# State products with g's high and low parts stacked on the partitions, half-row time order, and new instruction orders on all five queues

## The reference, cut to what matters

```python
x = x + (einsum('bnh,boh->bno', x, W[subject]) + b[subject])                 # layer 0
h = relu(x @ W1[lang] + b1[lang]); y = x + h @ W2[lang] + b2[lang]
x = x + layernorm(y) * gamma[lang] + beta[lang]                              # layer 1
# layer 2
ctx   = causal_ema(x, tau_ctx)
gated = x * sigmoid([x, ctx] @ Wg.T + bg)
h1    = gelu(x @ Wn1.T + bn1)
mod   = 0.5 + sigmoid(h1 @ Wn2.T + bn2)                                      # 32 values d per time
traces = vmap over d: causal_ema(gated * mod[d], tau[d])
temporal = sum_d softmax(blend)[d] * traces[d]
out = (gelu(x @ Wsoma.T + bsoma) * sigmoid(temporal @ Wtemp.T + btemp)) @ Wout.T
x = x + layernorm(out) * gamma2 + beta2
# layer 3: x = x + zX * (row second difference) + zY * (time second difference) + zR * x * (1 - x)
```

## Time and profile before

| | |
|---|---|
| Time, median of 3 runs | 1044.95 us (1042.16 to 1045.16) |
| Profiled execution, its own time | 1038.77 us |
| Span in that profile | 1037.0 us |
| Mean granted TensorE clock | 0.97 of full |
| TensorE, matrix products busy | 919.3 us, 89% |
| VectorE busy | 831.4 us, 80% |
| ScalarE busy | 392.7 us, 38% |
| GpSimd busy | 615.0 us, 59% |

### The profile page before, as it was taken

The page is one execution under the profiler, slowest core; times in us unless marked ns, Lnnn a source line. Parts: engine busy times, 40 slices in busy tenths (PEclk is TensorE's granted clock), DMA queues, the critical chain, the costliest instruction groups (busy, mean ns, idle before and its releaser), DMA issues.

```text
span 1037.0 us, 18886 instructions
## 1 busy us (share of the span) xinstructions
PE 919.3 (89%) x6088; PEld 776.7 (75%) x6088; DVE 831.4 (80%) x1333; ACT 392.7 (38%) x730; POOL 615.0 (59%) x654
## 2 busy tenths in 40 slices
PE   2678899999899999999999999999999999998961
PEld 1458697878778787878878787887878787887751
DVE  3788779797978979798888979698887969697762
ACT  3463433434243443434343342425343343424220
POOL 1445447484756668484766749475766748474523
PEclk9779999999999999999999999999999999999985
DMA  6664333534343343534454353434344353420011
GB/s 218 214 212 137 108 123 111 165 107 155 115 153 133 116 163 108 158 118 135 129 146 132 122 168 105 155 102 162 124 131 154 104 161 114 141 72 32 31 41 61
DMA packets 92815, 133.28 MB, mean 129 GB/s; under 512 B 15692, under 2 KB 32588, under 8 KB 92716
## 3 DMA queue, kind: packets, MB, share of 16 engines
q1 hardware_dynamic: 88372, 125.93, 38.9%
q10 hardware_dynamic: 4344, 6.14, 1.9%
HBM read 106.86 MB, written 8.39 MB: 111 GB/s over the span
## 4 chain that ended last, share of the span: by engine, by line
DVE 33%; issue 24%; POOL 19%; PE 16%; ACT 3%; DMA 2%; SPq 1%; ACTq 1%; POOLq 0%; DVEq 0%
PE bank L1241 6%; DVE work L998 5%; PE bank L1371 4%; DVE w_r L829 4%; POOL work L416 4%; POOL xh L391 3%; DVE work L1007 3%; POOL b_t L403 2%; PE bank L1233 2%; POOL work L452 2%; DVE work L1014 2%; DMA w_land<-in_L_cond_weight 2%; DVE amath L975 2%; DVE work L1068 2%; POOL work L457 2%
## 5 line engine op out<-in xcount | busy, mean ns | idle before, releaser
L416 POOL TENSOR_TENSOR work<-work 128x448 f32<-128x448 f32 (+3 forms) x224 | 200.3, 894 | 35.4 <-DVE work L998 18.5
L1241 PE MATMUL bank<-x2h,wg_r 128*128 128x256 f32 x1536 | 198.2, 284 | 12.8 <-DVE bank L946 12.8
L1241 PEld LDWEIGHTS bank<-x2h,wg_r 128*128 128x128 f32 x1536 | 185.8, 188 | 27.3 <-DVE bank L946 16.9
L1371 PE MATMUL bank<-gh,amath 128*128 128x512 f32 x384 | 106.1, 412 | 21.7 <-DVE work L998 17.2
L998 DVE TENSOR_TENSOR work<-bank,work 128x512 f32<-128x512 f32 (+7 forms) x256 | 105.1, 446 | 19.5 <-POOL work L416 14.0
L1233 PE MATMUL bank<-w_r,xh 128*128 128x512 f32 x384 | 106.2, 415 | 15.6 <-DVE w_r L829 11.3
L403 POOL TENSOR_TENSOR b_t<-b_t,work 128x512 f32<-128x512 f32 x32 | 51.8, 1618 | 107.9 <-DMA b_t<-in_L_cond_b 66.0
L1241 PE MATMUL bank<-x2h,wsoma_r 128*128 128x256 f32 x768 | 107.5, 289 | 3.7 <-ACT work L615 3.5
L1371 PEld LDWEIGHTS bank<-gh,amath 128*128 128x128 f32 x384 | 68.0, 190 | 55.6 <-DVE amath L975 16.3
L829 DVE TENSOR_TENSOR w_r<-w_land,w_r 128x1024 fp32r<-128x1024 f32 x64 | 85.5, 1337 | 26.6 <-ACT w_r L542 26.6
L1241 PEld LDWEIGHTS bank<-x2h,wsoma_r 128*128 128x128 f32 x768 | 94.4, 188 | 12.7 <-issue 7.2
(11 more groups left out here) (142 smaller groups left out, 1651.1 us busy)
## 6 DMA issues: line engine op xcount, KB each, us to landing
w_land<-in_L_cond_weight SPq DMA_DIRECT2D x64, 512.0 KB, 3.9
w_t<-in_L_cond_W SPq DMA_DIRECT2D x64, 256.0 KB, 3.2
work<-work SPq DMA_DIRECT2D x64, 224.0 KB, 2.5
work<-in_xT SPq DMA_DIRECT2D x32, 256.0 KB, 3.5
b_t<-in_L_cond_bias SPq DMA_DIRECT2D x32, 256.0 KB, 3.5
work<-in_x SPq DMA_DIRECT2D x32, 256.0 KB, 3.4
work<-in_L_cond_beta SPq DMA_DIRECT2D x32, 256.0 KB, 3.5
b_t<-in_L_cond_b SPq DMA_DIRECT2D x32, 256.0 KB, 3.3
```

The costliest lines, as they stand in the source:

```text
L416: g_.tensor_tensor(dst, dst, src, ALU.add).then_inc(S["acc_ready"], 1)
L1241: ins = mm(dst, weight[:, w_part, first_block + a, o * P:(o + 1) * P], act[:, x_part, a], start=(not onto and a + w_part + x_part == 0), s ...
L1371: ins = mm(STATES[r][s_][:, :], amath[:, a_part, s_ * P:(s_ + 1) * P], gh[:, g_part], start=(a_part + g_part == 0), stop=(a_part == 1))
```

## The change

**Time order.** Inside a row the 128 times were ordered by place in the chunk (8), then by chunk (16). Now each half row of 64 times has this order by itself: half (2), place in the chunk (8), chunk (8). All access patterns that turn one order into the other get one more level, and chunk terms are worked on as 8 runs of 8 x (8 - j) elements in place of 4 runs of 16 x (8 - j).

**States.** The states of groups 0 and 1 depend on the first 64 times only, which now are partitions 0 to 63. So `gh` gets a third part: its upper 64 partitions hold g's high part and its lower 64 the low part, both of the first half. The lower half of `amath`'s high part gets a second copy of its upper half for these two groups. One product over 128 partitions is then high x high plus high x low, and a second one over 64 partitions is low x high. Groups 2 and 3 stay as they were. ACT gets three new instructions per row: `g_top` and `g_bottom` (64 x 512) and `amat_dup` (64 x 256).

**Memory.** `h1T` and `m` share a buffer now, so `mod_hidden` on ACT has two more waits, and the reserved DMA scratch is 256 in place of 1024.

**Orders.** The lists of calls on all five queues are written anew.

```diff
+    HALVES = 2
+    KH = NK // HALVES
+    HT = T // HALVES
...
-        h1T, m_q = buf("h1T"), buf("m")
+        h1T = buf("h1T")
+        m_q = h1T
...
-        gh = sb("gh", [P, 2, C], f32r)
+        gh = sb("gh", [P, 3, C], f32r)
...
+            def g_top(p, r):
+                act.wait_ge(S["ghi_ready"], 2 * p + r + 1)
+                if 2 * p + r:
+                    act.wait_ge(S["state_done"], NG * (2 * p + r) - 2)
+                a_.activation(gh[0:P // 2, 2], gh[0:P // 2, 0].bitcast(f32), ACT.Copy).then_inc(S["gtop_ready"], 1)
+
+            def g_bottom(p, r):
+                act.wait_ge(S["glo_ready"], 2 * p + r + 1)
+                if 2 * p + r:
+                    act.wait_ge(S["state_done"], NG * (2 * p + r) - 2)
+                a_.activation(gh[P // 2:P, 2], gh[0:P // 2, 1].bitcast(f32), ACT.Copy).then_inc(S["gbottom_ready"], 1)
+
+            def amat_dup(p, r):
+                act.wait_ge(S["amathi_ready"], 2 * p + r + 1)
+                a_.activation(amath[P // 2:P, 0, 0:2 * P], amat[0:P // 2, 0:2 * P], ACT.Copy).then_inc(S["amatdup_ready"], 1)
...
             def state_weights_lo(p, r):
-                dve.wait_ge(S["amathi_ready"], 2 * p + r + 1)
+                dve.wait_ge(S["amatdup_ready"], 2 * p + r + 1)
...
                 for j in W_TILES[w]:
-                    width = NK * (Q - j)
-                    src = RING[n % 2][:, at_:at_ + 4 * width].rearrange("p (a r t) -> p a r t", a=2, r=2)
+                    width = KH * (Q - j)
+                    src = RING[n % 2][:, at_:at_ + 8 * width].rearrange("p (x t) -> p x t", x=8)
...
-                for a_part, g_part in ((0, 0), (0, 1), (1, 0)):
-                    ins = mm(STATES[r][s_][:, :], amath[:, a_part, s_ * P:(s_ + 1) * P], gh[:, g_part],
-                             start=(a_part + g_part == 0), stop=(a_part == 1))
+                cols_ = slice(s_ * P, (s_ + 1) * P)
+                if s_ == 0:
+                    pe.wait_ge(S["gtop_ready"], b + 1)
+                    pe.wait_ge(S["gbottom_ready"], b + 1)
+                if s_ < 2:
+                    mm(STATES[r][s_][:, :], amath[:, 0, cols_], gh[:, 2], start=True, stop=False)
+                    ins = mm(STATES[r][s_][:, :], amath[0:P // 2, 1, cols_], gh[0:P // 2, 0], start=False, stop=True)
+                else:
+                    for a_part, g_part in ((0, 0), (0, 1), (1, 0)):
+                        ins = mm(STATES[r][s_][:, :], amath[:, a_part, cols_], gh[:, g_part],
+                                 start=(a_part + g_part == 0), stop=(a_part == 1))
```

On SP, the calls behind `shift_rows(i, 0)` in a step are now these:

```diff
                     if live(i):
                         shift_rows(i, 0)
                     if live(i + 3):
-                        load_b0(i + 3, 0)
+                        load_b1(i + 3, 0)
+                        load_w1(i + 3, 0)
                         load_x(i + 3, 0)
```

More of the change, by code:

```diff
@@ L504, in _ @@
                 if live(i):
+                    quadratic(i, 0)
+                if live(i + 1):
+                    add_terms(i + 1, 9)
+                if i == -3:
+                    mask_spread()
+                if live(i + 3):
+                    x_plus_beta(i + 3, 0)
+                if live(i):
                     rstd(mv_c, rs_c, 2, i, 1)
                 if live(i + 3):
-                    x_plus_beta(i + 3, 0)
+                    x_lo(i + 3, 1)
+                if live(i):
+                    neighbours(i, 1)
+                if live(i + 3):
+                    x1_plus_b2(i + 3, 0)
                 if live(i + 2):
                     x2_plus_beta(i + 2, 1)
+                if live(i + 3):
+                    rstd(mv_a, rs_a, 1, i + 3, 0)
+                if live(i):
+                    row_neighbours(i, 1)
+                if live(i + 3):
+                    x_plus_b0(i + 3, 1)
+                if live(i):
+                    quadratic(i, 1)
+                if live(i + 3):
+                    x_plus_beta(i + 3, 1)
+                    x1_plus_b2(i + 3, 1)
+                if live(i + 2):
+                    add_terms(i + 2, 2)
+                    add_terms(i + 2, 3)
         @block.scalar
@@ L706, in _ @@
                     x1_turned(i + 2, 1)
-                if live(i + 3):
-                    w0_hi(i + 3, 0, 0)
                 if live(i + 1):
                     mod_rows(i + 1)
+                    amat_hi(i + 1, 0)
+                if i == -3:
+                    logs()
+                if live(i + 1):
+                    amat_dup(i + 1, 0)
                 if live(i + 2):
                     relu(i + 2, 1)
+                if i == -1:
+                    hi_parts(4)
+                if live(i + 3):
+                    x_hi(i + 3, 0)
+                if live(i + 1):
+                    soma_gelu(i + 1, 2)
+                    g_hi(i + 1, 0)
+                if live(i + 2):
+                    x2_hi(i + 2, 0)
+                if live(i + 1):
+                    soma_gelu(i + 1, 3)
+                    g_top(i + 1, 0)
+                    g_bottom(i + 1, 0)
+                if live(i + 3):
+                    w0_hi(i + 3, 0, 1)
+                if i == -3:
+                    exps()
+                if live(i + 2):
+                    x2_turned(i + 2, 0)
+                if live(i + 1):
+                    amat_hi(i + 1, 1)
+                    g_hi(i + 1, 1)
+                    amat_dup(i + 1, 1)
                 if i == -2:
@@ L1202, in _ @@
                 if live(i + 2):
-                    y_row(i + 2, 1)
+                    y_stats(i + 2, 1)
                 if live(i + 1):
-                    state_weights_lo(i + 1, 0)
-                    chunk_terms(i + 1, 6)
+                    g_lo(i + 1, 0)
                 if live(i + 2):
-                    y_stats(i + 2, 1)
+                    y_aggregate(i + 2, 1)
+                if live(i + 1):
+                    chunk_terms(i + 1, 8)
+                if live(i + 2):
+                    x2_lo(i + 2, 0)
+                    centred(i + 2, 1)
                 if live(i):
@@ L1478, in _ @@
                     tn_turn(i + 1, 1)
+                if i == -3:
+                    blend_rows()
                 if i == -2:
```

495 lines of the change are left out of this document (233 added, 262 removed).

## The result

The changed kernel takes 1067.6 us, median of 4 runs (1064.69 to 1068.75), against 1043.56 us (1039.01 to 1045.16) for the kernel before on the same chip: ratio 1.0233, 95% interval 1.0193 to 1.0274. It is slower by 2.3%; 1022 was forecast, and the range ended at 1057.

The account below looks back on a forecast made before the run. The prediction took a loop of TensorE (95% busy), VectorE and a side chain as the bound. A pair going from 58.96 to 57.4 us saves 1.56, times 15 = 23 us, from 1044.95: 1022 us, range 1010 to 1034 (8 in 10: 1001 to 1057).

Parts of the forecast that it names:

- third stretch: Row 0's `x3_row` to the next `temporal`: 13.9 us by the side chain, longer than VectorE's 13.1.
- side chain: Beside the third stretch: shifts, load of x, `x_plus_b0`, `quadratic`, last add, copy and turn ahead of `temporal`; 13.9 us.
- first stretch: Row 0's `temporal` to `y_row`, set by TensorE: 12.2 us against 10.77, one more `gate_ctx` standing ahead of the adapter.
- second stretch: VectorE's other work, between the first stretch and the third stretch: 29.3 us, with 0.6 of short waits 29.9.
- loop: The three stretches of a pair added up: 12.2 + 29.9 + 13.9 = 56.0 us.
- slower rival: Array shape changes in groups 0 and 1 cost 0.36 us each: 1074 us; chance 0.18, with smaller slips 0.21.
- my two signs of under 0.4 and of 1.4: Both first groups' time over 4 products: under 0.4 us more as forecast, 1.4 us if the slower rival holds.
- (a): Both last chunk weights ahead of `project`: 12 products cover the chunk terms, taking most of TensorE's 1.1 us a pair.
- (b): `final_sum` of row 1 behind all scans: VectorE's 2.7 us and TensorE's 0.8 us of idle time a pair go.
- moved wait: Shifts held by a load ahead of them, `temporal` waits for the last add: loop 57.5, 1044 us; chance 0.12.
- Start and tail: The span outside the repeated pairs, 152.6 us: no sure change, left at 0, give or take 5 us.
- the 1.4 us that I left idle: Half of TensorE's 2.9 us of idle time a pair, left on top of the loop: 57.4 us a pair.

Follow-up runs that it names:

- e4: The changed kernel with the load of x issued on SP right behind row 0's shifts, ahead of the loads of b1 and w1: 1025.57 us, ratio 0.9870.
- e6: e4 with the second stacked product over all 128 rows, the lower half of `amath`'s low part being zero: 1020.92 us, ratio 0.9809.
- e5: e4 with three products in the first two state groups and without the copies of g's parts: 1025.88 us, ratio 0.9842.
- e7: The changed kernel with the last add of the chunk terms ahead of `row_neighbours` and `quadratic` on GpSimd: 1064.34 us, ratio 1.0234.
- e9: The changed kernel, its loads left as they are, with the second stacked product over all 128 rows: 1065.84 us, ratio 1.0240.

## Why the prediction was wrong

**The step that failed** is the third stretch's term "two more small issues and the load of x at 0.3 to 0.5 each, 1.0". I took an issue for its own duration. In the changed kernel x's load starts 476.32 - 473.44 = 2.88 us behind the last shift. Each of the two small loads before it picks its source by an index; the first starts 1.23 us behind the last shift, the second 1.14 behind the first, and x, which has no index, 0.51 behind the second. The trace of before had it, SP behind the same shifts:

```profile
455.67 4.18 SPq L312 DMA_DIRECT2D work<-work  x6
461.06 0.36 SPq L273 DMA_DIRECT2D b_t<-in_L_cond_bias  x1
462.02 0.36 SPq L261 DMA_DIRECT2D work<-in_x  x1
```

There one small load puts x 2.2 us behind the shifts. With the start of x's issue at 2.9 in place of some 0.7, my side chain is 16.1; 15.2 was measured, since the landing, the three GpSimd operations and the hand-overs were a little shorter than my terms; in the pair shown the chain takes 14.8. e4 puts the price on this one step: with x's issue at 0.1 a pair is 3.2 us shorter, 57.2, and inside the forecast.

**The first stretch** was forecast at 12.2 and is 13.1 in the changed kernel, but 12.2 in e4 to e6: the sum of TensorE's work was right, and the extra 0.9 us is the late x again, by way of VectorE. The gate waits for two `th` instructions (L1069). They take 2.35 us in the changed kernel's pair, where a GpSimd instruction (L400) runs beside them, and 1.54 in e4's, where it starts behind them. Behind `temporal` at 484.06, TensorE's temporal gate starts at 488.99 after 0.64 us of waiting for VectorE, 4.93 us later; in e4 (582.02 and 585.87) it is 3.85.

**The second stretch** was forecast at 29.9 and is 31.5 to 32.2 in every kernel, 31.6 in the kernel before. This is a second step that failed, and it was a misreading: I took it as what is left of VectorE's 49.4 us a pair, and took the third stretch's share, 17.72, from one pair. That pair was the only one of its kind. Of the kernel before's 14 full pairs, the third stretch lasts 18.03 us in this one, 15.34 in the last and 16.12 to 16.15 in the twelve others, such as this one (columns as in the earlier trace rows):

```profile
515.66:531.80 16.14, 14.68 (x74) 9.67 (x72) 16.11 (x28) 5.96 (x10) 12.78 (x15) 1.00 0.48 132
```

Two VectorE instructions make the difference; in the pair above they take 0.84 and 1.21 us:

```profile
463.46 1.81 DVE L975 TENSOR_TENSOR amath<-work,amath 128x512 fp32r<-128x512 f32 x1 [0.31 <-ACT amath L629]
...
466.46 2.31 DVE L829 TENSOR_TENSOR w_r<-w_land,w_r 128x1024 fp32r<-128x1024 f32 x1
```

With 16.11 in place of 17.72 the second stretch is 49.4 - 7.4 - (16.11 - 3.98 - 1.0) = 30.9 us, with 0.6 of waits 31.5, as measured. The loop is then 57.6 and the pair 59.0 us: no gain at all would have been forecast. The wait of 1.16 us in the earlier trace rows, which I counted as unchanged, was of the same pair; it comes once in the whole middle.

VectorE's work did grow as well, from 49.8 us a pair (641.57 us busy in the window 140 to 900 before) to 646.69 / 760 x 60.4 = 51.4. No operation was added, but the mean of the `w_r` instructions, for one, went from 1337 to 1579 ns. The growth isn't what filled the second stretch: VectorE is busy there for 31.1 of 31.9 us, mean, and before's 27.5 with the 3.98 us moved there would be 31.5. The third stretch has most of it, 12.6 us in place of 11.1, and there VectorE waits anyway.

What lengthens them is seen where VectorE and GpSimd start side by side. In e4, and in the changed kernel:

```profile
573.76 1.80 DVE L1023 TENSOR_TENSOR amath<-work,amath 128x512 fp32r<-128x512 f32 x1
```
```profile
474.69 0.68 DVE L1023 TENSOR_TENSOR amath<-work,amath 128x512 fp32r<-128x512 f32 x1
```

Each starts within 0.02 us of GpSimd's L461 (573.74 and 474.68, above). In e4 GpSimd's takes 1.27 and VectorE's 1.80; in the changed kernel VectorE's takes 0.68 and GpSimd's 1.82. One of the two keeps its length, and the other gets longer. The Trainium skill (SBUF — State Buffer, Who interferes with whom) says that a VectorE instruction with two inputs in the on-chip memory contends with a GpSimd one that reads it. The two rows agree; which of the two waits, starts this close don't tell.

**TensorE's work.** 4 products less were to be 0.96 us; right by e6's 0.24 a product. A change of shape was taken at 0.1 and is 0.17, so the pair's 0.96 became 8 x 0.17 - 0.96 = 0.4 us more in place of 0.16 less. That sum of 6 us would have been the lesser part of the slower rival, and e5 shows it hidden: three products are as fast. The four products of the first two groups took 1.68 us, 0.7 over four plain ones, between my two signs of under 0.4 and of 1.4. The measured 0.17 lies between the 0.04 and the 0.36 that I had read at the spread. The Trainium skill (TensorEngine Tiling (Array Packing), Key Properties) says that a change of tiling mode drains TensorE. What the traces show of it is that the next weight load doesn't run ahead, 0.17 us. The Trainium skill (TensorE: Matmul & The Clock Gate, LDWEIGHTS) says that a load goes by columns and not by rows. The trace agrees: the 64-row loads take 183 ns, the 128-row ones 188.

**Waits removed.** (a) and (b) were right: `final_sum` waits no more in the middle, and the scans cost TensorE 1.6 us in the whole span. The chunk terms ahead of the states (1.1 us a pair) now cost 0.6 a pair, ahead of the chunk weights.

**A second wait overlooked.** I named `temporal` as what stands behind the last add. `out_centred(i, 1)` stands behind `quadratic`, and e7 shows that it alone holds the time. The sign that I gave for a moved wait, `row_neighbours` over 8 us behind `x3_row`, didn't appear: in the pair shown it starts 5.4 us behind, and the wait stands one place further on.

**The rivals.** The moved wait was the right one in kind ("held by a load ahead of them", GpSimd's queue, `temporal` takes it), with 0.12, and its loop of 57.5 came to 60.0: the first stretch is 0.9 longer, the second 1.8, the third 0.2 shorter. I had put the load ahead of the shifts; it was x's load behind them. That e4 came to 57.2 a pair, near the 57.4 forecast, is luck in part: its second stretch is 1.8 over the forecast, its third 0.8 under, and the 1.4 us that I left idle were not needed. Start and tail: 2.1, 5.0 (last period) and 0.8 us more, 7.9 together, outside "give or take 5". The last period fell to 51.4 us in e4, so part of it is the late x.

**What e4 against before is made of** isn't fully taken apart: 12.2 + 31.7 + 13.1 against 10.8 + 31.6 + 16.1 is 1.5 us a pair less. That this is what the moved work gives with x in time is argued, since no run moves one part of it alone.

## What to carry to other kernels

- Before a pair's stretch goes into a sum, compare it with the same stretch of other pairs. One pair with two lengthened instructions hid 1.6 us a pair here.
- Cost a transfer's issue by the distance from one issue's start to the next on its queue, not by its duration, and do it for every transfer that a list puts ahead of one on which the chain hangs.
- A transfer moved earlier brings its own wait with it: look at what frees its buffer before you put it ahead of others. In an in-order queue the wait is everyone's.
- Where an order is drawn up anew, list every instruction that waits for the late one, not just the first; freeing one of two (e7) gave nothing.

## What the hardware showed that I had not expected

- An alternation of 128 and 64 rows costs TensorE 0.17 us each time, by a weight load (183 to 188 ns) that doesn't run ahead. Filling the unused half with zeros removes it, here for one more VectorE instruction a row.
- A load whose source is picked by an index starts some 1.1 us behind the issue before it on SP, though its own row shows 0.35 to 0.41; one without an index starts 0.5 us behind.
- The granted clock fell behind long waits of TensorE. In the changed kernel one such wait of 3.19 us ends at 606.74:

```profile
606.74 0.66 PE L1278 MATMUL bank<-ident,work 128*128 128x128 f32 x4 [3.19 <-ACT work L675]
...
608.65 2.80 PE L1293 MATMUL bank<-x2h,wn_r 128*128 128x256 f32 x12
```

The window behind it, and the same 12 products in the pair without a fall:

```profile
608.60:612.00 3.40, 3.40 (x19) 3.40 (x18) 3.30 (x4) 2.12 (x4) 2.97 (x4) 0.53 0.00 0
```
```profile
485.29 1.66 PE L1293 MATMUL bank<-x2h,wn_r 128*128 128x256 f32 x12
```

The clock there is at its lower level, 1.2 GHz, and the products take 2.80 in place of 1.66 us. The clock's record has nine such pieces, 34 us in all, between 120 and 970 us of the changed kernel, none in the kernel before and one in e4. Seven of the nine begin within 2.3 us of row 0's `temporal`, where the turn's wait is. The ten middle pairs with such a piece take 60.5 us, median, the two without 59.6 and 59.9, so they may be some 0.7 us a pair, 6 us of the 30. e7 and e9 point the same way: with 14 and 48 us at the lower level their spans are 1063.0 and 1065.8 us. No run here holds the clock apart from the wait, so that share is argued and not shown.
